# GpSimd's join, power and key scaling in the last stage: a new order over chunks

## What is computed

```python
def attn_layer(x, Wqkv, qs, ksc, Wo):          # 16 heads of 64
    qkv = x @ Wqkv
    q, k, v = split into heads
    q = l2norm(q) * qs
    k = l2norm(k) * ksc
    q = q * cos * scale + rotate_half(q) * sin * scale
    k = k * cos * inv + rotate_half(k) * sin * inv
    out = local_attention(q, k, v)             # windows of 32, each sees itself and the one before
    return out @ Wo

for i in range(6):
    x = attn_layer(shift_tokens(x), Wqkv[i], q_scale[i], k_scale[i], Wo[i]) + x
    x = ffn_layer(shift_tokens(x), ...) + x    # layer norm, W1, gelu gate, W2
```

## Time and profile before

| | |
|---|---|
| three runs | 2320.69, 2322.05, 2334.29 us; median 2322.05 |
| the profiled execution | 2328.08 us, span 2326.2 |
| busy, of the span | TensorE 80%, VectorE 74%, ScalarE 55%, GpSimd 39% |
| GpSimd's joins, powers, scalings | 245.4, 354.8, 102.0 us busy (L1279, L1281, L1285) |
| VectorE's rotations L1567, L1568, L1569 | 146.6, 94.0, 82.0 us |
| VectorE's L1571 and L1573 | 129.5 and 93.2 us |

### The profile page before, as it was taken

How to read it: one execution, slowest core, us unless ns; L and a number is a source line. 1 busy time by engine, 2 the same in 40 slices (tenths; PEclk the granted TensorE clock), 3 DMA queues, 4 the chain that set the end, 5 groups by cost and what they waited for, 6 DMA issues and landing times. The chain is left out here.

```text
span 2326.2 us, 52273 instructions
## 1 busy us (share of the span) xinstructions
PE 1867.0 (80%) x18512; PEld 924.7 (40%) x18512; DVE 1716.5 (74%) x3041; ACT 1279.5 (55%) x1850; POOL 906.5 (39%) x913
## 2 busy tenths in 40 slices
PE   5745888888888888888846887887888888788786
PEld 3531222222222222222223654654655555555564
DVE  4744677767777777777648988878878887887893
ACT  4411665656666666666635655645546555555553
POOL 0012111111111111111028858648657666675670
PEclk9955898989999999999958998999999999999998
DMA  1002223232222232222004323323323333232330
GB/s 34 1 24 61 46 56 61 56 59 55 59 55 59 55 59 55 59 55 57 2 30 119 92 85 92 87 85 92 94 87 92 86 93 92 68 111 75 84 84 10
DMA packets 88745, 152.83 MB, mean 66 GB/s; under 512 B 16819, under 2 KB 51669, under 8 KB 84693
## 3 DMA queue, kind: packets, MB, share of 16 engines
q1 hardware_dynamic: 86421, 149.04, 26.2%
q10 hardware_dynamic: 2112, 0.94, 0.2%
HBM read 98.03 MB, written 51.12 MB: 64 GB/s over the span
## 5 line engine op out<-in xcount | busy, mean ns | idle before, releaser
L899 DVE TENSOR_REDUCE ENM<-PM 128x1 f32<-128x512 f32 x1024 | 658.4, 685 | 257.2 <-PE PM L722 248.8
L819 ACT ACTIVATE EPT<-PA 128x1024 f32<-128x1024 f32 x512 | 512.4, 1021 | 220.2 <-PE PA L734 137.6
L722 PE MATMUL PM<-EKX,EQX 48*128 48x512 bf16 x1024 | 356.3, 402 | 104.3 <-DVE ENM L899 84.0
L1279 POOL TENSOR_TENSOR DQR<-DR 128x512 f32<-128x512 f32 x192 | 245.4, 1278 | 289.0 <-DVE DR L1569 289.0
L1281 POOL TENSOR_TENSOR DRN<-DRN,DHALF 128x8 f32<-128x8 f32 x192 | 354.8, 1848 | 8.4
L642 POOL CAST ENMP<-ENM 128x16 bf16<-128x16 f32 x64 | 12.6, 196 | 786.2 <-DVE ENM L899 786.2
L744 PE MATMUL PV<-EPT,EVP 128*32 128x512 f32 x2048 | 286.7, 633 | 0.8 <-ACT EPT L819 0.7
L734 PE MATMUL PA<-EQX,EKX 51*128 51x512 bf16 x1024 | 254.8, 397 | 28.4 <-DMA EQX<-EROWS 15.9
L722 PEld LDWEIGHTS PM<-EKX,EQX 48*128 48x128 bf16 x1024 | 85.8, 95 | 482.1 <-DVE ENM L899 392.7
L1325 PE MATMUL PM<-DWQKV,DXS 128*128 128x512 f32 x384 | 218.0, 651 | 47.3 <-ACT XNT L1526 29.2
L1487 ACT ACTIVATE DRAW<-PM 128x512 f32<-128x512 f32 x192 | 114.7, 598 | 143.4 <-PE PM L1325 106.4
(11 more groups left out here) (208 smaller groups left out, 2960.9 us busy)
## 6 DMA issues: line engine op xcount, KB each, us to landing
DV<-d_vpark SPq DMA_DIRECT2D x192, 256.0 KB, 5.0
d_vpark<-DVT SPq DMA_DIRECT2D x48, 512.0 KB, 2.6
e_park<-EPARTS SPq DMA_DIRECT2D x64, 192.0 KB, 2.9
EQX<-e_park SPq DMA_DIRECT2D x32, 384.0 KB, 5.5
EKX<-e_park SPq DMA_DIRECT2D x32, 384.0 KB, 9.2
DWQKV<-in_WqkvR SPq DMA_DIRECT2D x6, 1536.0 KB, 9.5
e_park<-EPARTS SPq DMA_DIRECT2D x64, 128.0 KB, 2.7
e_park<-EPARTS SPq DMA_DIRECT2D x64, 64.0 KB, 2.1
```

The source lines that it names most:

```text
L722: pe.matmul(PM[:, r, :], lhsT=QX[64 * r:64 * r + KQ, b, hp, t * 128:(t + 1) * 128], rhs=KX[64 * r:64 * r + KQ, b, hp, :], start=True, stop ...
L819: s_.activation(PT[:, kt, pair * 2 * S:(pair + 1) * 2 * S], PA[:, 2 * pair:2 * pair + 2, :].rearrange("p a b -> p (a b)"), ACT.Exp, scale= ...
L899: v.tensor_reduce(NM[:, g % 2, t, j, 0:1], PM[:, r, :], AX.X, ALU.max, negate=True).then_inc(maxed, 1)
L1279: g.tensor_tensor(qr, r1, r2, ALU.add).then_inc(roped.sem if queries else joined.sem, 1)
```

## The change

GpSimd no longer does join, power and scaling of one chunk in one piece. Piece k now joins chunk k and then takes power and scaling of chunk k-1 (`norm_keys`); piece 32, which did nothing before, takes those of chunk 31. `joined` is now raised by all 32 joins, `roped` by the 16 key scalings alone. VectorE's rotation of chunk k waits for `joined` of chunk k-2. TensorE's transpose waits for `joined` with queries and for `roped` with keys.

```diff
-        joined, rooted = ev("joined", 2 * NT), ev("rooted", 4 * NT)
-        roped = ev("roped", 4 * NT, 2)
+        joined, rooted = ev("joined", 4 * NT, 2), ev("rooted", 4 * NT)
+        roped = ev("roped", 2 * NT)
...
+                def norm_keys(layer, k):
+
+                    n, c = divmod(k, 4)
+                    rn = RN[:, n % 2, 8 * c:8 * c + 8]
+                    pool.wait_ge(floored.sem, floored.at(layer, k))
+                    g.tensor_tensor(rn, rn, HALF[:, 0:8], ALU.pow).then_inc(rooted.sem, 1)
+                    if c >= 2:
+                        qr = QR[:, k % 4, :].rearrange("p (h e) -> p h e", h=8)
+                        pool.wait_ge(joined.sem, joined.at(layer, k))
+                        pool.wait_ge(rooted.sem, rooted.at(layer, k))
+                        g.tensor_tensor(qr, qr, bc(rn, 2, [128, 8, DL]), ALU.mult).then_inc(roped.sem, 1)
...
-                    elif name == "proj" and n[0] < NT:
+                    elif name == "proj":
                         k = 4 * n[0] + n[1]
-                        r1, r2 = (x[:, k % 2, :] for x in (R1, R2))
-                        rn = RN[:, n[0] % 2, 8 * n[1]:8 * n[1] + 8]
-                        qr = QR[:, k % 4, :]
-                        pool.wait_ge(rotated.sem, rotated.at(layer, k))
-                        pool.wait_ge(turned.sem, turned.at(layer, k - 4))
-                        queries = n[1] < 2
-                        g.tensor_tensor(qr, r1, r2, ALU.add).then_inc(roped.sem if queries else joined.sem, 1)
-                        pool.wait_ge(floored.sem, floored.at(layer, k))
-                        g.tensor_tensor(rn, rn, HALF[:, 0:8], ALU.pow).then_inc(rooted.sem, 1)
-                        if not queries:
-                            pool.wait_ge(joined.sem, joined.at(layer, 2 * n[0] + n[1] - 2))
-                            pool.wait_ge(rooted.sem, rooted.at(layer, k))
-                            g.tensor_tensor(qr.rearrange("p (h e) -> p h e", h=8), qr.rearrange("p (h e) -> p h e", h=8),
-                                            bc(rn, 2, [128, 8, DL]), ALU.mult).then_inc(roped.sem, 1)
+                        if k < 4 * NT:
+                            pool.wait_ge(rotated.sem, rotated.at(layer, k))
+                            pool.wait_ge(turned.sem, turned.at(layer, k - 4))
+                            g.tensor_tensor(QR[:, k % 4, :], R1[:, k % 2, :], R2[:, k % 2, :], ALU.add).then_inc(joined.sem, 1)
+                        if 0 < k <= 4 * NT:
+                            norm_keys(layer, k - 1)
...
-                            wait(roped, k - 4)
+                            if c < 2:
+                                wait(joined, k - 4)
+                            else:
+                                wait(roped, 2 * (n - 1) + c - 2)
...
-                        wait(roped, k - 2)
+                        wait(joined, k - 2)
```

More of the change, by code:

```diff
@@ L1261, in _ @@
                 pool.wait_ge(const, 32)
-                pool.sem_inc(roped.sem, roped.credit)
+                pool.sem_inc(joined.sem, joined.credit)
+                def norm_keys(layer, k):
[8 more added lines that the diff above has]
+                        g.tensor_tensor(qr, qr, bc(rn, 2, [128, 8, DL]), ALU.mult).then_inc(roped.sem, 1)
                 def piece(layer, name, n):
```

## The result

Over 20 runs of each, the changed kernel takes 2339.12 us in the median (2328.20 to 2349.61) and the kernel before 2328.77 (2314.51 to 2337.38): ratio 1.0049, 95% interval 1.0030 to 1.0067. It is slower by half a percent, some 11 us. The forecast was a small loss, 2335 on a median of 2322, a ratio of 1.0056. The profiled execution has a span of 2342.2 us against 2326.2, 16.0 us more for the 13 of the sum. Of all executions behind this document one, of the last kernel of experiment 8, took 4126.75 us for a reason that nothing here shows, and isn't counted.

A forecast was written before the change was run, and what follows sets the result against it. It took VectorE's own work to bound middle tiles, with GpSimd as full at a layer's start. Terms 0 + 9 + 4 gave +13 us on the profiled 2328.08, the same share giving 2335; 2305 to 2352 held about 8 in 10.

The forecast's parts named there:

- The start of a layer: First chunks of each layer, 6 times: removed wait and new hold-ups cancel, 0; at worst +0.7 us a layer.
- The middle tile: Three tiles a layer, 18 times: second join behind owed power and scaling, +0.5 us each; total +9, up to +16.
- RSTD: Feed-forward's power, 12 times: 1.2 us later, 0.35 left after part is given back; +4 us, or +14 with nothing back.
- TensorE: Transpose of key chunk 7: TensorE stands about 2 us once a layer, covered, so 0; without cover +13 us.
- The wait gone: New profile: VectorE's idle before L1574 that ends at the key scaling, 9.6 us in the run before, should be gone.
- GpSimd's idle time ahead of joins: New profile: total about as large as before, with a gap behind nearly every first chunk of a layer.
- Middle tiles 17.5 to 18.1: New profile: tiles in the middle of a layer should last 17.5 to 18.1 us for 17.2.
- Normalisation's idle time: New profile: VectorE's idle before the normalisation should rise, at 1428.67 from 2.32 us to about 3.5.
- The floor's mean rising from 486 ns: New profile: the mean time of VectorE's floor instruction should rise from 486 ns.
- The freed wait pays: Rival at a layer's start: wait and hold-ups come back, -17 us, 2305; gains given 0.12 short of 1%, 0.06 beyond.
- Nothing moves: Rival for the whole kernel: hold-ups trade evenly and RSTD's delay is covered, 2322 (-4 to +4 us); chance 0.18.
- TensorE and RSTD held up: Slower rival: deferred scaling holds up TensorE at chunk 7 and RSTD; +30 us, 2352, deciding from about 23; chance 0.17.

The follow-up runs named there:

- last kernel of experiment 8: Kernel before with its old order, VectorE waiting for joins alone, floor folded into the sum and RSTD ahead of the power: ratio 0.9753 to the kernel before.
- experiment 1: Kernel before with only the semaphore waits moved, GpSimd keeping its old order of join, power and scaling: ratio 1.0008 to the kernel before.
- experiment 4: Changed kernel with RSTD ahead of the owed power and scaling of chunk 28 (8 for the second batch): ratio 0.9972 to the kernel before.
- experiment 5: Kernel before, old order kept, with RSTD ahead of the power of chunk 29 (9 for the second batch): ratio 0.9976 to the kernel before.
- experiment 6: Changed kernel with RSTD first, plus power and scaling of chunk 7 done at once: ratio 0.9988 to the kernel before.
- experiment 3: Changed kernel with nothing owed across a tile's end, the last chunk's piece doing its own power and scaling too: ratio 1.0124 to the kernel before.

## Why the prediction was right, point by point

The tile times, slot by slot (mean of layers 1 to 4, us; tile 7 to the next layer's first rotation):

| tile | 0 | 1 | 2 | 3 | 4 | 5 | 6 | 7 | sum |
|---|---|---|---|---|---|---|---|---|---|
| before | 13.44 | 19.09 | 21.91 | 27.65 | 17.26 | 17.18 | 17.58 | 47.48 | 181.6 |
| changed | 13.86 | 18.48 | 22.12 | 27.05 | 17.62 | 17.86 | 18.95 | 47.73 | 183.7 |
| forecast difference | 0 for both | | +0.35 | 0 | +0.5 | +0.5 | +0.5 | +0.35 | +2.2 |
| measured | +0.42 | -0.61 | +0.21 | -0.60 | +0.36 | +0.68 | +1.37 | +0.25 | +2.1 |

The time came out inside the forecast, and the steps below show the mechanism as it was worked out. But the means of the table hold something that the forecast had not: TensorE's granted clock. Where it stays at 1.00, and TensorE doesn't pause, a tile repeats to 0.03 us over the layers 1 to 5; where it falls, the tile is longer. The changed kernel's tile 6 in layers 1 and 3 and a piece of the first of these, then tile 1 of the kernel before in layers 1 and 4 (stretch, length, the five engines, clock, DMA):

```profile
1504.53:1525.02 20.49, 15.48 (x189) 10.47 (x188) 17.21 (x30) 8.21 (x16) 15.14 (x10) 0.83 0.30 79
1874.53:1892.40 17.87, 16.34 (x298) 11.67 (x294) 17.32 (x29) 11.69 (x22) 15.16 (x10) 1.00 0.33 90
1520.00:1523.40 3.40, 3.40 (x13) 2.26 (x11) 1.12 (x1) 1.57 (x3) 0.04 (x1) 0.50 0.00 0
...
1401.83:1421.34 19.51, 16.55 (x235) 10.95 (x226) 15.01 (x28) 9.79 (x20) 16.72 (x12) 0.91 0.40 110
1947.23:1965.59 18.36, 15.40 (x237) 10.04 (x227) 16.17 (x27) 10.20 (x21) 16.71 (x12) 1.00 0.44 119
```

From 1520.00 to 1523.40 the clock is at its lower level, 1.2 of 2.4 GHz. Slot 3 does the same in both kernels: 25.96 us in two layers of each, at a clock of 0.90 to 0.93, and up to 28.2 (before) and 28.6 (changed) in the others, at 0.82 to 0.88. With the shortest of the layers 1 to 5 in each slot, the differences are +0.42 and +0.12 for the first two tiles, +0.21, 0, then +0.35, +0.68, +0.67, and +0.34 to the rotation of tile 7's last chunk.

*The start of a layer.* Forecast: R(3) later by 1.05, R(4) by 0.44, R(5) earlier by 0.14, in sum nothing. Measured in the layer of the earlier trace rows, from its first rotation: +1.03, +0.41, -0.76, then R(6) +0.60, and R(8) -0.60; in the mean of four layers -0.2 over both tiles. The wait was removed and the hold-ups took its place, as the step said and as experiment 1 shows by itself, one chunk later than I had it. The -0.60 is the kernel before at a fallen clock (the row of 19.51 us above); in the layers 4 and 5, where both kernels have 1.00, R(8) is 0.54 late. So the term was +3 us rather than 0, inside the +0.7 a layer that I gave as the worst.

*The middle tile.* Forecast: the third chunk 1.1 late by a join that has slipped behind the owed power and scaling, the tile 0.5 longer. The timeline of tile 5, VectorE and then GpSimd:

```profile
1488.57 0.42 DVE L1575 TENSOR_TENSOR DR<-DRAW,DTAB 128x256 f32<-128x256 f32 x1
...
1491.25 0.68 DVE L1574 TENSOR_TENSOR DR<-DRAW,DTAB 128x512 f32<-128x512 f32 x1
1491.85 1.50 DVE L1575 TENSOR_TENSOR DR<-DRAW,DTAB 128x256 f32<-128x256 f32 x1
...
1487.98 2.18 POOL L1268 TENSOR_TENSOR DRN<-DRN,DHALF 128x8 f32<-128x8 f32 x1
1490.31 1.05 POOL L1273 TENSOR_TENSOR DQR<-DQR,DRN 128x512 f32<-128x512 f32 x1
1491.31 1.75 POOL L1288 TENSOR_TENSOR DQR<-DR 128x512 f32<-128x512 f32 x1
```

Owed power, owed scaling and the second join follow each other as worked out. In one detail it was otherwise: I had 4.60 us for L1574 and 4.55 for the join (5.82 less 1.27), a matter of 0.05, and VectorE was first. The join then waits for L1574 (1.75 us for 1.27), and the half rotation L1575 waits for the join (1.50 for 0.42). The third chunk ends 1.1 us late all the same (4.37 us behind the second, for 3.29), and 0.54 of it comes back behind the fourth (7.21 for 7.75), whose floors are held up 27 times for 41. L1575 has 33 rows over 0.6 us where the old L1568 had 15; the 18 more, one for each middle tile, account for most of the 21 us by which it grew. At full clock the three middle tiles lose 0.35, 0.68 and 0.67 us, some +10 over the run for the forecast's +9.

Tile 6's +1.37 in the table is more than that. TensorE pauses amid the transposes of `P` ahead of tile 7's first projection:

```profile
1519.74 1.47 PE L144 MATMUL PA<-IDENT,DP 128*128 128x128 f32 x7 [2.97 <-issue]
```

The kernel of experiment 1, with the old order, has the same pause at the same place:

```profile
1515.53 0.93 PE L144 MATMUL PA<-IDENT,DP 128*128 128x128 f32 x7 [3.71 <-issue]
```

"issue" says that TensorE waited for nothing that the profile shows. The changed kernel pauses there in layers 1 to 5 (2.97, 2.48, 1.25, 3.18 and 3.05 us), the kernel before in 1, 3, 4 and 5 (1.30, 2.96, 2.41 and 1.32). The pause alone costs tile 6 at most 0.3 us (17.87 us in layer 4 of the changed kernel, 17.93 in layer 5 of experiment 4's after a pause of 3.47, 17.48 for 17.20 in layer 3 of the kernel before), and up to 0.8 at the next chunk. Where the granted clock falls directly behind it, the tile is long: 20.49, 19.56 and 20.71 us in layers 1, 2 and 5, and in the kernel before 18.45 in layer 4. So the pause isn't the new order's alone. What it is stays open, and so does whether the new order makes the clock fall more often: there is one profile of each kernel. Over all executions on record the mean granted clock of a run is 0.915 for the changed kernel (20 executions), 0.920 for the kernel before (63, on three chips) and 0.918 for experiment 4's, and within each kernel the executions with the lower clock tend to be the longer ones. Some of the measured 11 us may thus be the clock's; no run separates it.

*RSTD.* Forecast: 1.2 us later. At chunk 9 RSTD now starts 4.83 us behind its rotation in all five layers, for 3.64: +1.19. The step to chunk 10 is 1.19 longer (8.91 for 7.72), the next 0.84 shorter (4.07 for 4.91), as worked out, and the one behind it 0.14: +0.21 in the slot, for 0.35. At chunk 29 the delay is between -0.39 and +1.20, small where the pause had already held up chunk 29; in layer 3, where nothing did, the two steps come to +1.19 and -0.85, +0.34 together. By these rows the term was some +3 us for +4. Experiments 4 and 5 agree: their edit is worth 4.5 us more in the new order than in the old at the steps that hold RSTD. That the whole of experiment 4 gains 18 us and of experiment 5 only 5.6, not clear of nothing, leaves room for more (12 us, give or take 10), but the rows of experiment 4 put the surplus at steps ahead of RSTD, where the clock differed.

So the terms at full clock are some +3 for 0, +10 for +9 and +3 for +4: about +16 for +13. That the profiled pair came out at 16.0 as well is in part luck. Pauses and the fallen clock cost the kernel before some 10 us in slots 1 and 3 and 3 us in tile 6 and ahead of chunk 29, the changed kernel 7 us in slot 3 and 12 in tile 6 and ahead of chunk 29. None of this was in the sum, and it was made up for, since RSTD's delay is partly hidden where chunk 29 is held up anyway, and the first layer doesn't repeat the others.

*TensorE.* Forecast: some 2 us once a layer at chunk 7, covered. The row is there, 2.92 us:

```profile
1425.71 1.12 PE L144 MATMUL PX<-IDENT,DQR 128*128 128x128 f32 x4 [2.92 <-POOL DQR L1273]
```

and experiment 6 shows that VectorE's reading of the score is no later for it.

*What I said of the new profile.* The wait gone: yes. GpSimd's idle time ahead of joins about as large, but in more places: yes, 308.6 us in 87 places for 289.0 in 77. Middle tiles 17.5 to 18.1: yes at full clock (17.6, 17.9 and 17.9), not where the clock fell. Normalisation's idle time at the layer of the earlier trace rows from 2.32 to about 3.5: it went to 2.59, since VectorE's own variance step now was held up by the join (1.09 us for 0.17) and used up the time. The floor's mean rising from 486 ns: no, it is 466. Of the 192 floors 103 were held up (over 0.3 us) and 101 are now: behind a tile's second chunk 10 for 3, where joins at a layer's start do meet floors, behind the first 47 for 42, but behind the fourth only 27 for 41. The new order moves hold-ups from the fourth floor and the subtraction to rotations rather than adding them at the floor; when nothing is owed, the floors do pay (experiment 3).

*The rivals.* "The freed wait pays" fell with experiment 1. "Nothing moves" is outside the interval, though only by 0.3%. "TensorE and RSTD held up": TensorE's half is refuted by experiment 6. RSTD's half needed nothing to be given back, and 0.84 of 1.19 us is, one step later; the whole stayed under the 23 us from which that case decides.

## What to carry to other kernels

Removing a wait between two engines that hold each other up was worth nothing here while both had work: look for where the instruction goes next, not only at the idle time it leaves. When work is deferred on an engine, ask first which short and urgent instruction (here a power of 4 values, RSTD) now stands behind it; putting that one ahead took 10.9 us off the steps that hold it, about as much as the reordering had added at the middle tiles. A short instruction whose mean is several times its shortest row was the better target than either order: the floor of 8 values a row cost 93.2 us of 2326, and folding it into the sum gave 2.3%. And before a difference of two tile times is put down to an edit, compare the granted clock of the two stretches: at 1.00 the tiles here repeat to 0.03 us, and a fall moved them by more than the edit did.

## What the runs showed of the hardware

- An instruction on VectorE of 8 values a row (170 ns) waits for the end of a whole join of 1.27 us on GpSimd if it starts inside it; the same floor as a reduce doesn't. This is the rule of the Trainium skill, "SBUF — State Buffer", section "Who interferes with whom", that whichever starts first keeps the shared port pair and the other is blocked; the trace agrees, with 0.74 us in the median of the kernel before's 192 floors, for 0.17. It goes both ways: a join took 1.75 us for 1.27 behind an L1574.
- I had not expected that the engines would take turns: L1574, join, L1575, each behind the other, and in the stretches shown neither engine gets two instructions through while the other is waiting. In experiment 1 the same is seen with scaling, half rotation, join, half rotation (1.40, 1.26, 1.45 and 1.49 us).
- GpSimd's power costs 1.65 us for 8 values a row and 1.0 for 4, and up to 2.18 beside a rotation on VectorE, where it is stretched but doesn't hold VectorE up (L1575 took its 0.42 us inside the 2.18).
- TensorE's granted clock fell from 1.00 to 0.50 from 1520.00 to 1523.40, right behind a pause of 2.97 us, and the tile took 20.49 us for 17.87. A pause of 3.47 us at the same place in layer 5 of experiment 4's kernel was followed by no fall within the tile, and the tile took 17.93.
